# Down products of the last experts as three matmuls of rounded parts and rests, and the last token list made a slot ahead

## What is computed

```python
norm = layer_norm(feat, ln_g, ln_b)                 # 2048 x 256
scores = norm @ centroids.T                         # 2048 x 8
# expert 0 takes its 256 best rows, expert 1 the 256 best of the rest, ...
for e in range(E):
    s = jnp.where(taken, -jnp.inf, scores[:, e])
    _, idx = jax.lax.top_k(s, C)
    taken = taken.at[idx].set(True)
h = layer_norm(routed, ln_g, ln_b)                  # 8 x 256 x 256
h = gelu(einsum('ecd,edf->ecf', h, w1) + b1)        # 8 x 256 x 1024
h = einsum('ecf,efd->ecd', h, w2) + b2              # 8 x 256 x 256
out = routed + h                                    # back to the rows' places
```

## Time and profile before

| | us |
|---|---|
| median of three runs | 327.42 (326.5 to 328.05) |
| the profiled execution | 326.79 |
| its span, first to last instruction | 324.3 |
| TensorE matmuls busy (share) | 291.0 (90%) |
| VectorE busy | 219.4 (68%) |
| GpSimd busy | 178.0 (55%) |
| ScalarE busy | 145.1 (45%) |

### The profile page before, as it was taken

The page is one execution under the profiler, slowest core; times in us unless marked ns, Lnnn a source line. Parts: engine busy times, 40 slices in busy tenths (PEclk is TensorE's granted clock), DMA queues, the critical chain, the costliest instruction groups (busy, mean ns, idle before and its releaser), DMA issues.

```text
span 324.3 us, 6529 instructions
## 1 busy us (share of the span) xinstructions
PE 291.0 (90%) x2080; PEld 251.1 (77%) x2081; DVE 219.4 (68%) x749; ACT 145.1 (45%) x266; POOL 178.0 (55%) x240
## 2 busy tenths in 40 slices
PE   8999998999999999998831599999999999999990
PEld 3999887999989999997820267787878787888890
DVE  0679999788888887888368867878787878311000
ACT  1366564455545546555441244353535353532420
POOL 8100444455566656544516335758686868787831
PEclk9999999999999999999975599999999999999997
DMA  7992005930001000000112301646455556543010
GB/s 267 351 381 102 2 0 182 389 111 35 32 32 65 32 32 32 32 32 35 65 65 60 114 23 32 197 131 192 166 187 174 180 179 188 178 145 106 17 65 16
DMA packets 21623, 37.50 MB, mean 116 GB/s; under 512 B 2400, under 2 KB 14944, under 8 KB 21216
## 3 DMA queue, kind: packets, MB, share of 16 engines
q1 hardware_dynamic: 19040, 30.89, 27.4%
q0 software_dynamic: 2560, 6.31, 6.5%
HBM read 30.90 MB, written 6.29 MB: 115 GB/s over the span
## 4 chain that ended last, share of the span: by engine, by line
PE 76%; DVE 12%; issue 4%; ACT 2%; POOL 2%; DMA 1%; DVEq 0%; POOLq 0%; ACTq 0%
PE pair L908 67%; PE pair L991 4%; DVE cmpb L773 3%; PE pair L958 2%; DVE pair L806 2%; PE pair L1097 1%; POOL yT L441 1%; DMA G<-rows_scratch,idx 1%; PE pair L1020 1%; DVE ok L793 1%; DVE wneg L623 1%; ACT yT L573 1%; POOL out_dram L456 1%; PE pair L1063 1%; ACT pT L532 1%
## 5 line engine op out<-in xcount | busy, mean ns | idle before, releaser
L908 PE MATMUL pair<-w2s,hT 128*128 128x256 f32 x256 | 63.2, 387 | 0.0
L908 PE MATMUL pair<-yT,w1p 128*128 128x256 f32 x384 | 53.9, 290 | 1.6 <-POOL yT L441 1.6
L381 POOL TENSOR_TENSOR pr<-pr,rs 128x1024 f32<-128x1024 f32 x16 | 31.7, 1979 | 42.0 <-DVE rs L714 42.0
L908 PE MATMUL pair<-Bm,pT 128*128 (+1 forms) x384 | 50.0, 285 | 2.3 <-DVE pT L707 2.3
L908 PEld LDWEIGHTS pair<-yT,w1p 128*128 128x128 f32 x384 | 48.2, 189 | 4.2 <-POOL yT L441 2.1
L908 PEld LDWEIGHTS pair<-w2s,hT 128*128 128x128 f32 x256 | 45.7, 191 | 4.6
L908 PEld LDWEIGHTS pair<-Bm,pT 128*128 128x128 f32 x384 | 47.0, 188 | 2.7 <-issue 2.7
L908 PE MATMUL pair<-Am,xTp 128*128 (+1 forms) x192 | 48.8, 402 | 0.0
L435 POOL TENSOR_TENSOR w1p<-w1s,w1p 128x512 fp32r<-128x512 f32 x32 | 40.0, 1274 | 5.4 <-ACT w1p L562 5.3
L583 ACT ACTIVATE hT<-pair,b1s 128x256 f32<-128x256 f32 x64 | 26.9, 471 | 34.7 <-PE pair L908 34.1
L908 PEld LDWEIGHTS pair<-Am,xTp 128*128 128x128 f32 x192 | 34.9, 188 | 7.4
(11 more groups left out here) (132 smaller groups left out, 527.9 us busy)
## 6 DMA issues: line engine op xcount, KB each, us to landing
w1s<-w_dram SPq DMA_DIRECT2D x8, 1024.0 KB
w2s<-w_dram SPq DMA_DIRECT2D x8, 1024.0 KB, 7.5
rows_scratch<-row SPq DMA_DIRECT2D x16, 256.0 KB, 2.0
xs<-x_dram SPq DMA_DIRECT2D x1, 2048.0 KB, 16.9
xTs<-xT_dram SPq DMA_DIRECT2D x1, 2048.0 KB, 18.6
wk_s<-wk_dram SPq DMA_DIRECT2D x1, 1024.0 KB, 5.2
wv_s<-wv_dram SPq DMA_DIRECT2D x1, 1024.0 KB, 7.3
wqT_s<-wqT_dram SPq DMA_DIRECT2D x2, 512.0 KB, 9.0
```

The costliest lines, as they stand in the source:

```text
L381: pool_mul = nc.gpsimd.tensor_tensor(p4, p4, rs[:, v, :].unsqueeze(1).unsqueeze(3).to_broadcast([P, KG, H, K8]), ALU.mult)
L908: return nc.tensor.matmul(out_, l, r, start=start, stop=stop)
```

## The change

All down products of experts 6 and 7, and of expert 5 those of blocks f = 4 to 7, are made by `mm3` from parts and rests of hT and w2s. For this ScalarE rounds halves of w2 (`w2_high`), VectorE makes their rests (`w2_rest`), and VectorE makes part and rest of each pair of hidden blocks (`hidden_split`). The parts of w2 lie where the inputs xs and xTs lay, which are no longer needed then; the parts of the hidden blocks, hp, in space that was unused.

The list of expert 7 is made in slot 7 in place of slot 8: VectorE's part follows the selection in round 3 and its indices stand between the new instructions at the slot's end, TensorE's are in gaps 8 and 9, ScalarE's is behind hidden(6, 0), and GpSimd's token_rows and gather stand behind y_rest(6) and bias(6). The transposes of expert 7's rows move one gap ahead, to gaps 3 and 4 of slot 8.

```diff
+        def parted(e, f):
+            return e > PARTED or e == PARTED and f >= FC // 2
+        def w2_parts(e, half):
+            return 1 if e == PARTED else 2 * (e - PARTED) + half
+        def hidden_parts(e, g):
+            return g - 1 if e == PARTED else FC // 2 * (e - PARTED) - 1 + g
+        PARTED = E - 3
 # GpSimd, slot with e = k - 1
-                    token_rows(e)
+                    if e < E - 1:
+                        token_rows(e)
...
-                    gather(e)
+                    if e < E - 1:
+                        gather(e)
...
                     y_rest(e, v)
+                    if e == E - 2:
+                        token_rows(E - 1)
                     bias(e)
+                    if e == E - 2:
+                        gather(E - 1)
 # ScalarE
+            def w2_high(e, half):
+                act.wait_ge(e_w2[e % 2], 16 * (e // 2 + 1))
+                if e >= PARTED + 2:
+                    act.wait_ge(e_o, ST * (e - 1))
+                q = slice(half * FC // 2, (half + 1) * FC // 2)
+                nc.scalar.activation(w2p[:, (e - PARTED) % 2, 0, q], w2s[:, e % 2, q], ACT.Copy).then_inc(e_w2h, 1)
...
                     rows(u, u % 2)
+                    if u >= PARTED:
+                        w2_high(u, 1 if u == PARTED else 0)
                     for g in range(first_part(u) // 2):
                         hidden(u, u % 2, g)
+                        if u == E - 2 and g == 0:
+                            lists_out(E - 1)
+                    if u > PARTED:
+                        w2_high(u, 1)
 # VectorE
+            def w2_rest(e, half):
+                dve.wait_ge(e_w2h, w2_parts(e, half))
+                q, b = slice(half * FC // 2, (half + 1) * FC // 2), (e - PARTED) % 2
+                nc.vector.tensor_tensor(w2p[:, b, 1, q], w2s[:, e % 2, q], w2p[:, b, 0, q].bitcast(f32),
+                                        ALU.subtract).then_inc(e_w2l, 1)
+            def hidden_split(e, g):
+                q = slice(2 * g, 2 * g + 2)
+                dve.wait_ge(e_hs, FC * e + 2 * g + 2)
+                if e > PARTED:
+                    dve.wait_ge(e_o, ST * e)
+                nc.vector.tensor_copy(hp[:, 0, q], hT[:, e % 2, q]).then_inc(e_hh, 1)
+                dve.wait_ge(e_hh, hidden_parts(e, g))
+                nc.vector.tensor_tensor(hp[:, 1, q], hT[:, e % 2, q], hp[:, 0, q].bitcast(f32), ALU.subtract).then_inc(e_hl, 1)
...
+                    if r == 0 and PARTED <= k - 2 < E:
+                        hidden_split(k - 2, 2)
+                        if k - 2 == PARTED:
+                            w2_rest(PARTED, 1)
-                    if r == 1 and 0 <= u < E:
+                    if r == 1 and 0 <= u < E - 1:
                         indices(u)
+                    if r == 1 and PARTED <= k - 2 < E:
+                        hidden_split(k - 2, 3)
                     if r == 2 and 0 <= k - 3 < E:
                         final(k - 3, 1)
                     if r == 3 and k == E - 1:
                         select(k)
+                        lists(k)
+                        one_hot(k, 0, Loh, r_loh)
...
+                if PARTED < u < E:
+                    w2_rest(u, 0)
+                    hidden_split(u, 0)
+                    if u == E - 2:
+                        indices(E - 1)
+                    w2_rest(u, 1)
+                    hidden_split(u, 1)
 # TensorE, in down(e, n)
                 if a == 0:
-                    pe.wait_ge(e_hs, FC * e + f + 1)
-                last = mm(bank[4 + a][:, 0:C], hT[:, v, f, a * P:(a + 1) * P], w2s[:, v, f, :], f == 0, f == FC - 1)
+                    if parted(e, f):
+                        pe.wait_ge(e_w2l, w2_parts(e, f // (FC // 2)))
+                        pe.wait_ge(e_hl, hidden_parts(e, f // 2))
+                    else:
+                        pe.wait_ge(e_hs, FC * e + f + 1)
+                if parted(e, f):
+                    last = mm3(bank[4 + a][:, 0:C], lambda i: hp[:, i, f, a * P:(a + 1) * P],
+                               lambda i: w2p[:, (e - PARTED) % 2, i, f, :], f == 0, f == FC - 1)
+                else:
+                    last = mm(bank[4 + a][:, 0:C], hT[:, v, f, a * P:(a + 1) * P], w2s[:, v, f, :], f == 0, f == FC - 1)
 # TensorE, the slots
-                        if r in (4, 5):
-                            rows(u, r - 4)
+                        at = 3 if u == E - 1 else 4
+                        if r in (at, at + 1):
+                            rows(u, r - at)
...
+                if k == E - 1:
+                    tokens(k)
                 expert_part(k, 9)
+                if k == E - 1:
+                    spread(k)
```

More of the change, by code:

```diff
@@ L80, in build @@
         step_w = cst[:, C_W:C_W + ROUNDS * NT].rearrange("p (r j) -> p r j", r=ROUNDS)
-        xs = sb("xs", [P, T, C])
-        xTs = sb("xTs", [P, CC, B * Q])
+        with ExitStack() as inputs:
+            xs = sb("xs", [P, T, C], f32, inputs)
+            xTs = sb("xTs", [P, CC, B * Q], f32, inputs)
+        w2p = sb("w2p", [P, 2, 2, FC, C], f32r)
         wneg = sb("wneg", [P, HD // P])
@@ L98, in build @@
         hT = sb("hT", [P, 2, FC, CAP])
-        sb("rest_of_factors", [P, 2 * B * CC * COLS + 2 * GROUPS * C - 2 * GB * ST * C - 5 * CC * CAP - 2 * FC * CAP])
+        hp = sb("hp", [P, 2, FC, CAP], f32r)
+        sb("rest_of_factors", [P, 2 * B * CC * COLS + 2 * GROUPS * C - 2 * GB * ST * C - 5 * CC * CAP - 4 * FC * CAP])
         bst = sb("bst", [P, T, 6])
@@ L181, in build @@
         e_gT, e_yT, e_yl, e_h, e_hs = sem("rows_transposed"), sem("rowsT_copied"), sem("rowsT_rest"), sem("hidden_in_psum"), sem("hidden_made")
+        e_w2h, e_w2l, e_hh, e_hl = sem("w2_high"), sem("w2_rest"), sem("hidden_high"), sem("hidden_rest")
         e_o, e_rb, e_fin = sem("expert_out"), sem("residual_bias"), sem("rows_final")
@@ L584, in hidden, with lists_out @@
                                          bias=b1s[:, e * FC + f:e * FC + f + 1]).then_inc(e_hs, 1)
+            def w2_high(e, half):
[4 more added lines that the diff above has]
+                nc.scalar.activation(w2p[:, (e - PARTED) % 2, 0, q], w2s[:, e % 2, q], ACT.Copy).then_inc(e_w2h, 1)
+            def lists_out(u):
+                act.wait_ge(r_R, u + 1)
+                nc.scalar.activation(Rt[:], bank[3][0:LO, 0:LO], ACT.Copy).then_inc(r_Rt, 1)
             act.wait_ge(s_in["small"], 64)
@@ L594, in _ @@
                     hidden(e, e % 2, g)
-                if 0 <= u < E:
-                    act.wait_ge(r_R, u + 1)
-                    nc.scalar.activation(Rt[:], bank[3][0:LO, 0:LO], ACT.Copy).then_inc(r_Rt, 1)
+                if 0 <= u < E - 1:
+                    lists_out(u)
                 for g in rest[1:]:
@@ L875, in indices, with lists @@
                                             ALU.add).then_inc(r_idx, 1)
+            def w2_rest(e, half):
[11 more added lines that the diff above has]
+                nc.vector.tensor_tensor(hp[:, 1, q], hT[:, e % 2, q], hp[:, 0, q].bitcast(f32), ALU.subtract).then_inc(e_hl, 1)
+            def lists(u):
+                slots(u)
+                halves(u)
+                one_hot(u, 1, Hoh, r_hoh)
             nc.vector.tensor_copy(M[:], S[:, 0, :].unsqueeze(1).to_broadcast([P, NT, T])).then_inc(r_m, 1)
@@ L880, in _ @@
                 u = k - 1
[L881 to L884, removed]
+                if 0 <= u < E - 1:
+                    lists(u)
                 for r in range(ROUNDS):
@@ L889, in _ @@
                             keep(k, r - 1)
-                    if r == 0 and 0 <= u < E:
+                    if r == 0 and 0 <= u < E - 1:
                         one_hot(u, 0, Loh, r_loh)
-                    if r == 1 and 0 <= u < E:
+                    if r == 0 and PARTED <= k - 2 < E:
[3 more added lines that the diff above has]
+                    if r == 1 and 0 <= u < E - 1:
                         indices(u)
+                    if r == 1 and PARTED <= k - 2 < E:
+                        hidden_split(k - 2, 3)
                     if r == 2 and 0 <= k - 3 < E:
@@ L1163, in list_of_tokens @@
                 u = k - 1
-                if gap == 1 and 0 <= u < E:
+                if gap == 1 and 0 <= u < E - 1:
                     if half == 0:
```

## The result

The changed kernel takes 332.39 us (median; 331.85 to 332.57) against 327.43 before: a ratio of 1.0156, with a 95% interval of 1.0135 to 1.0178. It is slower, as forecast, but by 5.0 us and not by 2.0, and its time lies 0.4 us above the range. In a later run, beside other kernels, the same program took 330.38 (ratio 1.0094, 1.0072 to 1.0116). The profiled execution took 332.42 us with a span of 330.6, 6.3 more than the span before. Of these, 1.0 lies ahead of slot 7, in the part that the change doesn't touch: tokens(6) starts at 279.10 instead of 278.10, 0.56 of it with the first loads and the rest in slot 1.

A forecast was written before the change was run, and what follows sets the result against it. The prediction took the tail as bound by TensorE, closely followed by a gather, a ScalarE-GpSimd chain and GpSimd's queue. Terms 1.10 + 0.08 + 0.81 = +1.99 on 327.42 gave 329.4 us (profiled execution 328.8), range 326.4 to 332.0.

The forecast's parts named there:

- the cost of the products: Down products in slots 7 to 9: 0.367 us as three matmuls against 0.442, at most 3.0 us saved over 40.
- the term of slot 8: Expert 6 down, expert 7 up: GpSimd's queue behind the moved gather and scatter decides, +0.08 us (bounds -0.3 and +0.4).
- Slot 7: Expert 5 down, expert 6 up: VectorE's new work delays indices(6) and the gather, +1.10 us (bounds +1.0 and +1.3).
- rival 1: VectorE and GpSimd exclude each other: 2.5 us above the sum, 331.9, or 331.1 with two thirds; chance 0.25.
- My third price: Third place where VectorE and GpSimd would meet: w2_rest(7, 0), 1.22 us, ready at just the time of y_rest(7).
- the 0.9 ahead of indices(7): Slot 8, if VectorE and GpSimd exclude each other: the splits meet y_rest, bias and gathers, some 0.9 us.
- Slot 9: Expert 7 down: TensorE waits for VectorE's parts at f = 2, 4 and 6, +0.81 us (bounds +0.5 and +1.2).
- my middle value of 0.57: VectorE's rounded 128x512 copy in hidden_split, taken at 0.57 us between 0.44 (same kind) and 0.68 (same size and type).
- the last sentence of the prediction: A granted clock below full in the last 40 us would be something not counted; no size given.
- Edits at nothing: ScalarE's w2_high copies fit into its idle time and the new buffers lie where unread inputs lay: no cost.
- Rivals 2 and 3: Two: VectorE's parts keep ahead of TensorE, 326.1, chance 0.18. Three: three matmuls cost no less, 330.0, chance 0.05.

The follow-up runs named there:

- indices_first: Changed kernel with indices(6) ahead of w2_rest(5, 1) on VectorE: 329.24 us, ratio 1.0076; its profiled execution took 332.12 us.
- no_parts_of_5: Changed kernel without parts for expert 5, with GpSimd's work reordered and w2_rest(7, 0) waiting for y_rest(7): 327.28 us, ratio 1.0002.
- psum_operand: Changed kernel with a constant PSUM column as second operand of VectorE's new instructions (results wrong, for times only): 329.54 us, ratio 1.0072.
- filler: Changed kernel with 16 unused matmuls on TensorE in the idle stretch ahead of up(7, 0): 330.35 us, ratio 1.0099.
- three_repairs: Changed kernel with indices(6) first, two parts of w1_rest(7) ahead of gather(7), and w2_rest(7, 0) behind y_rest(7): 328.00 us, ratio 1.0045.
- halves_late: Changed kernel with parts only for blocks f = 4 to 7 of experts 6 and 7, GpSimd reordered, w2_rest(7) behind y_rest(7): 328.31 us, ratio 1.0031.
- w1_first: Changed kernel with w1_rest(7, 0) ahead of gather(7) on GpSimd: 331.52 us, ratio 1.0144; its profiled execution took 329.80 us.

## Why the prediction was right and wrong

- **What bounds the kernel, and the cost of the products**: right. 40 products at three matmuls were cheaper as counted, and none of it reached the end in the changed kernel.
- **The step that failed** is the term of slot 8, +0.08. It takes every duration of GpSimd from the undisturbed rows, although VectorE's new instructions run beside them; that the two engines hold each other up was put at nothing. Measured was +2.75, of which 2.4 are this. What followed from it, the lowered clock behind a longer idle time, had no term at all and cost 1.24 in slot 9.
- **Slot 7**, forecast +1.10, measured +1.20. The row after has the indices behind w2_rest (281.93 behind 280.80) and TensorE waiting 0.44 for the gather. That ranks(7) is next to be late was right too: it waits 0.60 at 283.92, and indices_first regained only 0.38. no_parts_of_5 shows the whole term.
- **Slot 8**, forecast +0.08 at the second channel and so 15.7 at the first, 0.3 over before. The mechanism, GpSimd's queue behind the moved gather and scatter, was right in place and size: without the exclusion it took 15.76. In it the four w1_rest begin 9.91 after up(6, 0), where I had 9.84; in the changed kernel it is 11.31. The prediction had written of rival 1 "For it: GpSimd decides slot 8 by my own count. Against: nothing but the missing row.", and yet gave it 0.25 and no part of the sum. My third price was right, w2_rest(7, 0) meets y_rest(7) for 1.0 us; the 0.9 ahead of indices(7) was 0.25 (the gather starts 5.30 after up(6, 0), 5.05 in psum_operand). The rest, 1.15, is the second gather (1.42) and the scatters (1.15, 1.51), which meet VectorE's instructions behind indices(7); there the rival had no price.
- **Slot 9**, forecast +0.58 counted from the first channel (+0.81 at the second), measured +1.41. The waits for VectorE are there (0.71 at f = 2; later ones are inside the run of 42 records). With the copy at 0.69, as psum_operand has it, slot 9 is 14.32, 0.93 over before, and my count gives the same within 0.1. The copy is 0.42 when nobody interferes, so the row of the same kind (0.44) was the right one, and my middle value of 0.57 was neither. With 0.42 the count gives +0.16, and the three kernels at full clock with this copy (filler, three_repairs, no_parts_of_5) have +0.17 or +0.18. So the term was 0.4 too high, and that hid a part of what the clock added. What was missing is the clock: the last sentence of the prediction named it as something not counted, and it cost 1.24 us.
- **Edits at nothing**: right for ScalarE. w2_rest(6, 0) and (7, 0), for which the sum has no term, were not free: they met bias and y_rest.
- **The sum for the profiled execution**: forecast 328.8, measured 332.42. The 3.6 us between them are, rounded, 0.1 in slot 7, 2.5 in slot 8, 0.8 in slot 9 and 1.0 ahead of slot 7, less 0.7 outside the span, which the prediction took as fixed at 2.5. The last two are no part of any term and cancel in part, by luck.
- **Range and chances**: slower was right. Rival 1 was the case that came, near its price of 2.5 (2.4 in slot 8, and 0.28 on one copy in slot 7), plus 1.2 for the clock, which follows from it and which its range didn't hold: an idle time of 3.6 us where my count had 1.1 is paid twice. The second run of the same program, 330.38, would have been within the range, by the same mechanism.
- **Rivals 2 and 3**: out. No part of VectorE was faster than its rows. Matmuls of w2p and hp that follow one another without a wait go as fast as the ups: in the second profile of the changed kernel 21 of them take 2.72 us and 6 take 0.87, so 15 more cost 1.85, 0.123 each; of the ups of the earlier trace rows 45 take 5.66 and 39 take 4.94, 0.120 each.

```profile
300.92 2.72 PE L986 MATMUL pair<-w2p,hp 128*128 128x256 f32 x21
```

## What to carry to other kernels

Work given to an idle engine is not free by its duration alone: ask with which operands it runs beside which other engine, and where a wait on it falls. A rule of the hardware that speaks against a change belongs in the sum, not only among the rivals, when nothing in the trace contradicts it and the engine concerned is the one that decides a stage. Two changes that are each worth nothing, here an earlier list and cheaper products, can be worth 3 us when both limits of a stage are lifted together, here with the order of GpSimd's queue and the place of an operand set to match.

## What was not expected of the hardware

- The engine that is shut out doesn't wait for one instruction only. A copy of 0.42 us lasted 3.37 us beside two GpSimd instructions behind one another, and w2_rest of 1.22 lasted 4.55; which side gets in differs between executions of one program.
- TensorE's granted clock was 0.55 in the 3.8 us behind an idle time of 3.59 us, and 0.53, 0.72 and 0.75 in the 3.6 us behind idle times of 2.33 (halves_late), 2.66 and 2.10, so about the lower level for all or a part of them. It stayed full behind two of 0.87 and 1.01 with three matmuls between them in w1_first. The Trainium skill, TensorE: Matmul & The Clock Gate, section What's actually happening, says that activity, not rest, is what opens the clock; the filler, which only kept TensorE active, agrees.
